# Moving the last two layer norms of the second attention out of its stage, in a four-stage transformer kernel

## The reference

```python
x = layernorm(x + attn1(x))              # no gain or shift, eps 1e-5
# attn1: one head of width 128; Q, K, V from 128x128 weights; out = softmax(Q K^T / s) V
#        out = transpose(out, (0, 2, 1)).reshape(B, S, D); return out @ wo.T
# ffn1, on h = x of the line above:
normed = h * rsqrt(mean(h * h) + 1e-8) * norm_weight
shared = relu(normed @ sw1 + sb1) @ sw2 + sb2                 # 128 -> 512 -> 128
probs  = sigmoid(normed @ router_w.T)                         # 8 experts
w, idx = top_k(probs, 2); w = w / (sum(w) + 1e-6)
routed = sum over experts e of comb[:, e] * (relu(normed @ ew1[e] + eb1[e]) @ ew2[e] + eb2[e])
x = layernorm(h + shared + routed)
```

## Time and profile before

| | |
|---|---|
| three runs, median (lowest to highest) | 1117.27 us (1116.45 to 1118.58) |
| the profiled execution's own time | 1117.38 us |
| its span, first to last instruction | 1115.6 us |
| mean granted TensorE clock | 0.971 of 2.4 GHz |
| busy: PE, DVE, ACT, POOL | 1038.6, 839.0, 652.1, 683.8 us |
| `attend_once` in the trace | about 769 to 877.5 us |
| `mix_experts` in the trace | 878.0 us to the end |

### The profile page before, as it was taken

One profiled execution on the slowest core, in us unless ns is written; L12 is line 12 of the kernel. 1 busy time (PEld: TensorE's weight loads), 2 busy tenths in 40 slices (PEclk: granted clock), 3 DMA queues, 4 the chain that ended last, 5 costly groups with the idle time before them and its releaser, 6 DMA issues. The chain is left out here.

```text
span 1115.6 us, 25325 instructions
## 1 busy us (share of the span) xinstructions
PE 1038.6 (93%) x7983; PEld 855.6 (77%) x7983; DVE 839.0 (75%) x1699; ACT 652.1 (58%) x1319; POOL 683.8 (61%) x663
## 2 busy tenths in 40 slices
PE   6799999999999999999999999687997599999996
PEld 4678888888888888888888888455685477777774
DVE  5877887877787787787787787355765569888896
ACT  4556565565555555656565565454444587766774
POOL 4166876876876876777777786401221277767772
PEclk9999999999999999999999999988898799999998
DMA  5243533533633533534534433110000011212111
GB/s 125 51 97 75 123 85 71 130 78 71 130 79 74 129 78 80 120 78 88 112 78 97 107 75 67 32 42 1 0 1 1 20 60 63 88 56 75 57 38 38
DMA packets 57041, 80.09 MB, mean 72 GB/s; under 512 B 25956, under 2 KB 38048, under 8 KB 55968
## 3 DMA queue, kind: packets, MB, share of 16 engines
q1 hardware_dynamic: 54780, 78.97, 30.0%
q10 hardware_dynamic: 2220, 0.59, 0.3%
HBM read 19.43 MB, written 1.11 MB: 18 GB/s over the span
## 5 line engine op out<-in xcount | busy, mean ns | idle before, releaser
L617 POOL TENSOR_TENSOR probs_lo<-probs 128x512 f16<-128x512 f32 x384 | 420.1, 1108 | 195.2 <-ACT probs L450 193.5
L481 DVE TENSOR_REDUCE maxes<-bank_m 128x1 f32<-128x512 f32 x512 | 353.0, 690 | 138.2 <-PE bank_m L288 134.4
L450 ACT ACTIVATE probs<-bank_s 128x512 f32<-128x512 f32 x512 | 296.9, 608 | 266.1 <-PE bank_s L376 265.3
L369 PE MATMUL bank_s<-qa,ka 128*128 128x512 f32 x512 | 226.0, 441 | 5.7 <-DVE v_parts L528 2.5
L288 PE MATMUL bank_m<-ka,qa 128*128 128x512 f32 x512 | 204.9, 400 | 3.6 <-DMA ka<-tk_lo 3.3
L376 PE MATMUL bank_s<-qb,kb 65*128 65x512 f32 x512 | 205.8, 402 | 2.2 <-DMA qb<-negmax 2.2
L311 PE MATMUL bank_o<-v_now,probs 128*128 128x129 f16 x2048 | 200.6, 220 | 1.0 <-ACT o_parts L416 1.0
L1368 POOL TENSOR_TENSOR hidden_lo<-rectified,hidden_hi 128x512 fp32r<-128x512 f32 x112 | 155.6, 1406 | 60.7 <-ACT hidden_hi L1513 49.9
L311 PEld LDWEIGHTS bank_o<-v_now,probs 128*128 128x128 bf16 x2048 | 175.4, 97 | 21.9 <-issue 20.6
L307 PE MATMUL bank_o<-v_now,probs_lo 128*128 128x65 f16 x2048 | 184.7, 193 | 0.0
L288 PEld LDWEIGHTS bank_m<-ka,qa 128*128 128x128 f32 x512 | 158.6, 310 | 28.6 <-DMA ka<-tk_lo 3.7
(11 more groups left out here) (250 smaller groups left out, 1681.6 us busy)
## 6 DMA issues: line engine op xcount, KB each, us to landing
qa<-tq_hi SPq DMA_DIRECT2D x64, 256.0 KB, 3.8
v_now<-v_parts SPq DMA_DIRECT2D x32, 260.0 KB, 2.3
ka<-tk_hi SPq DMA_DIRECT2D x32, 256.0 KB, 2.9
ka<-tk_lo SPq DMA_DIRECT2D x32, 256.0 KB, 4.9
kb<-tk_hi SPq DMA_DIRECT2D x32, 256.0 KB, 5.0
qb<-tq_lo SPq DMA_DIRECT2D x32, 256.0 KB, 5.2
gates_on_all<-gate_rows SPq DMA_DIRECT2D x8, 1024.0 KB, 4.7
e_raw<-in_L_ffn_ew_dram SPq DMA_DIRECT2D x16, 256.0 KB, 3.0
```

The source lines that it names most:

```text
L369: nc.tensor.matmul(bank_s[u % 2][:], ka[h][:, ks], qa[h][:, qs], start=True, stop=False)
L450: nc.scalar.activation(probs[:, c, u, :], bank_s[u % 2][:], ACT.Exp, scale=SCALE).then_inc(exp_done, 1)
L481: nc.vector.tensor_reduce(maxes[:, j // 2, j % 2:j % 2 + 1], bank_m[j % 2][:], AX.X, ALU.max).then_inc(m_reduced, 1)
L617: nc.gpsimd.tensor_tensor(probs_lo[:, c, u, :], p, hi, ALU.subtract).then_inc(lo_pool, 1)
```

## The change

The work on a chunk's layer norm is cut in four functions, and each part gets another place.

- In step 3 only `times_wo(0)`, `times_wo(1)` and `add_and_sum` (the addition and moments) remain. The roots of chunks 0 and 1 stand on ACT behind the last exponential. `normalise_tokens(0)` and `(1)` stand on DVE in the fifth pass, behind quarters 0 and 1. The normalised `X` is now written by GpSimd, with two 128x512 instructions for a chunk (`normalise_input`), whose second operand is broadcast along the row.
- PE turns chunk 0 of `n_tok` in the fifth pass between its third and fourth quarter, ACT takes it out there, and DVE makes its `nt_lo` last.
- `times_wo`, moments, roots and normalisation of chunks 2 and 3 move to `mix_experts`: PE begins with `times_wo(2)`, turning of chunk 1, `times_wo(3)`. It turns chunks 2 and 3 behind chunks 0 and 1 of ffn 0; DVE, not ACT, takes them out.
- `route()` moves behind chunk 1 and `turn_gates()` behind chunk 3 of ffn 0. The memset of `gates[0]` stands behind the two `normalise_tokens`.
- GpSimd normalises `X` of chunks 2 and 3 behind its work for ffn 0.
- Statistics buffers get a place for each chunk. `o_new`, `w_t`, `nt`, `nt_hi`, `nt_lo` and the semaphores outlive the block.

```diff
@@ attend_once, GpSimd
+            for c in range(EARLY):
+                normalise_input(nc, pool, X, ln, c)
@@ attend_once, PE
-            for c in range(CK // 2, CK):
-                times_wo(c)
+                    if step == STEPS and kt == TB - 3:
+                        turn_tokens(0)
@@ attend_once, ACT
-                    if (step, kt - 1) in FINISH_AT:
-                        root(FINISH_AT[step, kt - 1])
-            for c in range(CK // 2, CK):
-                root(c)
+                    if step == STEPS and kt == TB - 3:
+                        act.wait_ge(ln["n_turned"], 1)
+                        nc.scalar.activation(nt[:, 0:CH], bank_a[0][:], ACT.Copy, scale=nw).then_inc(ln["nt_ready"], 1)
...
+                if step == STEPS - 1:
+                    act.wait_ge(eps_set, 2)
+                    for c in range(EARLY):
+                        root_of_variance(nc, act, ln, c, EPS_RMS)
@@ attend_once, DVE
-                    if (step, kt - 1) in FINISH_AT:
-                        finish(FINISH_AT[step, kt - 1])
-            for c in range(CK // 2, CK):
-                finish(c)
-            dve.wait_ge(x_done, CK)
+                    if (step, kt - 1) in WO_AT:
+                        c = WO_AT[step, kt - 1]
+                        add_and_sum(nc, dve, X, ln, c, bank_m[c % 2])
+                    if step == STEPS and kt in (1, 3):
+                        normalise_tokens(nc, dve, X, persist["n_tok"], ln, kt // 2)
...
@@ mix_experts
-        GATES_AT = 2
+        ROUTE_AT, GATES_AT = 1, 3
+        LATE = CK // 2
@@ mix_experts, GpSimd, after its 16 units of ffn 0
+                if first_ffn:
+                    for c in range(LATE, CK):
+                        normalise_input(nc, pool, X, ln, c)
@@ mix_experts, PE
-                    if first_ffn and c == 0:
+                    if first_ffn and c + 2 < CK:
+                        turn_tokens(c + 2)
+                    if first_ffn and c == ROUTE_AT:
                         route()
...
+            times_wo(LATE)
+            turn_tokens(1)
+            for c in range(LATE + 1, CK):
+                times_wo(c)
             over_ffns(pe, ffn)
@@ mix_experts, ACT
+            act.wait_ge(turned, 2)
+            nc.scalar.activation(nt[:, CH:2 * CH], bank_y[1][:], ACT.Copy, scale=nw).then_inc(nt_ready, 1)
+            take_hi(1)
+            root_of_variance(nc, act, ln, LATE, 1e-8)
...
+                            if c == 0 and f == 1:
+                                root_of_variance(nc, act, ln, LATE + 1, 1e-8)
+                            if c < 2 and f == 3:
+                                take_hi(c + 2)
@@ mix_experts, DVE
+            add_and_sum(nc, dve, X, ln, LATE, bank_y[LATE])
+            take_lo(1)
+            add_and_sum(nc, dve, X, ln, LATE + 1, bank_y[LATE + 1])
+            for c in range(LATE, CK):
+                normalise_tokens(nc, dve, X, n_tok, ln, c)
+            nc.vector.memset(gates[0][:], 1.0).then_inc(gates_in[0], 16)
+            for c in range(LATE, CK):
+                dve.wait_ge(turned, c + 1)
+                nc.vector.tensor_scalar(nt[:, c * CH:(c + 1) * CH], bank_y[c][:], nw, None, ALU.mult).then_inc(nt_ready, 1)
+                take_lo(c)
@@ new
+def normalise_input(nc, pool, X, ln, c):
+    x = X[:, 4 * c:4 * c + 4, :]
+    wide = lambda ap: ap.unsqueeze(2).broadcast_to((P, 4, P))
+    pool.wait_ge(ln["n_ready"], c + 1)
...
+    nc.gpsimd.tensor_tensor(x, x, wide(ln["mv"][:, c, :, 0]), ALU.subtract).then_inc(ln["done"], 1)
+    pool.wait_ge(ln["done"], 2 * c + 1)
+    nc.gpsimd.tensor_tensor(x, x, wide(ln["rstd"][:, c, 0, :]), ALU.mult).then_inc(ln["done"], 1)
```

More of the change, by code:

```diff
@@ L944, in attend_once @@
         o_hi = sb("o_hi", [P, 2, P])
-        o_new = sb("o_new", [P, S])
+        o_new = persist["o_new"]
         bank_a = [ps(f"bank_a{i}") for i in range(4)]
@@ L951, in attend_once @@
         SMALL = small.shape[1]
[L952 to L956, removed]
+        nw = small[:, SMALL - 1:SMALL]
+        ln = persist["ln"]
+        eps, eps_set = ln["eps"], ln["eps_set"]
+        nt, nt_hi, nt_lo = persist["nt"], persist["nt_hi"], persist["nt_lo"]
         shared_hi, shared_lo = sem("shared_hi_ready"), sem("shared_lo_ready")
@@ L1182, in reduce @@
                                             negate=True).then_inc(c_ready, 1)
[L1183 to L1205, removed]
             for n in range(AHEAD):
@@ L1373, in _, with times_wo, turn_tokens @@
         def _(pe):
-            for c in range(CK):
+            def times_wo(c):
+                for j in range(4):
+                    t = 4 * c + j
+                    last = nc.tensor.matmul(bank_y[c][:, j * P:(j + 1) * P], persist["o_new"][:, t * P:(t + 1) * P],
+                                            persist["w_t"][:, 3, :], start=True, stop=True)
+                last.then_inc(ln["y1_filled"], 1)
+            def turn_tokens(c):
+                pe.wait_ge(ln["n_ready"], c + 1)
                 for j in range(4):
@@ L1410, in second_product @@
                     pe.wait_ge(lo_dve, lo_dve_count(n, c))
-                if f == 0 and not first_ffn:
+                if f == 0 and first_ffn:
+                    pe.wait_ge(nt_ready, c + 1)
+                elif f == 0:
                     pe.wait_ge(y_taken, CK * (n - 1) + c + 1)
@@ L1431, in put_input @@
                 pe.wait_ge(comb_t_ready, CK)
+                pe.wait_ge(ln["done"], 2 * CK)
                 pe.wait_ge(y_taken, CK * NE + 2)
@@ L1556, in _, with take_lo @@
             nc.vector.memset(eps[:], 1e-5).then_inc(eps_set, 1)
-            nc.vector.memset(gates[0][:], 1.0).then_inc(gates_in[0], 16)
-            for c in range(CK):
+            def take_lo(c):
                 cs = slice(c * CH, (c + 1) * CH)
@@ L1714, in build @@
         quantised_ffn(nc, a, persist)
+        CK = T // 4
+        persist["o_new"], persist["w_t"] = sb("o_new", [P, B * S], F32), sb("w_turned", [P, 4, P], F32)
+        persist["nt"] = sb("nt", [P, B * S], F32)
+        for which in ("nt_hi", "nt_lo"):
+            persist[which] = sb(which, [P, B * S], F32R)
+        ln = {"stats": sb("ln_attn_stats", [P, CK, 4, 6], F32), "mv": sb("ln_attn_mean_var", [P, CK, 4, 2], F32),
+              "std": sb("ln_attn_std", [P, CK, 2, 4], F32), "rstd": sb("ln_attn_rstd", [P, CK, 2, 4], F32),
+              "eps": sb("attn_eps", [P, 2], F32)}
@@ new lines, in root_of_variance, with normalise_tokens @@
+def root_of_variance(nc, act, ln, c, eps_rms):
+    act.wait_ge(ln["moments"], c + 1)
+    nc.scalar.activation(ln["std"][:, c, 1, :], ln["mv"][:, c, :, 1], ACT.Sqrt, bias=ln["eps"][:, 1:2], scale=1.0 + eps_rms)
+    nc.scalar.activation(ln["std"][:, c, 0, :], ln["mv"][:, c, :, 1], ACT.Sqrt, bias=ln["eps"][:, 0:1]).then_inc(ln["rooted"], 1)
+def normalise_tokens(nc, dve, X, n_tok, ln, c):
+    dve.wait_ge(ln["rooted"], c + 1)
+    nc.vector.reciprocal(ln["rstd"][:, c, :, :], ln["std"][:, c, :, :]).then_inc(ln["inverted"], 1)
+    dve.wait_ge(ln["inverted"], c + 1)
+    for j in range(4):
+        t = 4 * c + j
+        last = nc.vector.tensor_scalar(n_tok[:, t, :], X[:, t, :], ln["mv"][:, c, j, 0:1], ln["rstd"][:, c, 1, j:j + 1],
+                                       ALU.subtract, ALU.mult)
+    last.then_inc(ln["n_ready"], 1)
```

63 lines of the change are left out of this document (41 added, 22 removed).

## The result

The changed kernel took 1109.86 us (median of 5 runs, 1109.72 to 1112.65); the kernel before took 1117.27 us beside it. The ratio is 0.9938, with a 95% interval of 0.9923 to 0.9953: faster by 0.6%, 7.4 us. The forecast was 1109.2 us. One execution of the kernel with both edits, further down, took 5615.5 us and is left out of its time.

The account below looks back on a forecast made before the run. One serial chain from 849.8 to 884.1 us, with PE gaps of 7.26 and 9.47 us, was taken as the bound. 15.9 - 6.8 - 1.0 = 8.1 us off 1117.38 gave 1109.2 us; own range 1107 to 1111.5, with rivals 1104 to 1113.5.

Parts of the forecast that it names:

- Step A: attend_once: fifth pass starts 6.9 us earlier, PE idle some 0.9 us; block ends 15.9 us earlier.
- Rivals 3 and 4: 3: attend_once gains much less, 1116 us, chance 0.08. 4: slow GpSimd broadcast instruction, kernel slower, chance 0.05.
- Step B: Opening of mix_experts: first relu at 4.65 us, ACT starts chunk 1 at 16.4 us from the block's start.
- disputed term: Opening of mix_experts: DVE's normalise_tokens wait out running GpSimd instructions, 3.9 us; chunk 1 at 16.4 instead of 12.6 us.
- Rival 1: DVE meets GpSimd rarely in chunk 0: chunk 1 starts near 12.6 us, loss 3.0 us, total 1105 us; chance 0.22.
- Step C: ffn 0 from chunk 1 through the router: ffn 1 starts 40.7 us after the block's start, loss 6.8 us.
- rival 2: PE's clock falls in ffn 0 behind a 2 to 3 us gap: 3 to 4 us more, 1112.5 us; chance 0.20.
- signs of being wrong: Forecast wrong if the block starts after 864, or ffn 1 more than 43 or less than 38 us behind it.
- the router and GpSimd's pairs: Expected signs: route in ffn 0 at 3.7 us; GpSimd's pairs normalising X at 1.2 to 1.4 us an instruction.
- Step D: ffn 1: GpSimd's four new instructions delay its first hidden_lo; loss 1.0 us, between 0 and 2.

Follow-up runs that it names:

- kernel with both edits: Changed kernel with gates memset at the expert block's front and GpSimd's remainders behind the last normalise_tokens: 1102.5 us, again 1105.41 us.
- roots back: Changed kernel with the roots of chunks 0 and 1 back in step 3 and normalise_tokens right behind each moment set: 1116.01 us, ratio 0.9992.
- GpSimd-waits run: Changed kernel with one added wait: GpSimd begins the shared expert's remainders only when all n_tokens are normalised: 1102.52 us, again 1100.92 us.
- warm-products run: Changed kernel with 15 extra unused 512-column products in PE's gap inside chunk 1 of the shared expert: 1109.66 us, ratio 0.9912.
- memset-first run: Changed kernel with DVE's memset of the first gates moved to the front of the expert block: 1105.26 us, ratio 0.9883.
- first-stage-only run: Changed kernel with chunks 2 and 3 finished at the end of attend_once, router and gates behind chunks 0 and 2 again: 1109.56 us, ratio 0.9919.

## Why the prediction was right, and where it was lucky

The sum was 15.9 - 6.8 - 1.0 = 8.1 us; the spans differ by 7.7 us, which the table splits as 1.1 + 17.5 - 10.65 - 0.25.

**Step A** came out at 17.5 instead of 15.9 us. The mechanism is shown: roots back, and 7.9 us of it are gone with PE's gap. PE restarts with 0.43 us idle and keeps its clock. The 1.6 us too little are a size: I added durations end to end, while in the rows most DVE instructions start about 0.1 us before the one ahead of them ends (854.31 + 1.84 = 856.15, the next starts at 856.07), over a dozen in a row, and I started 0.3 us late. GpSimd's broadcast instruction took 1.04 to 1.07 us here, less than the 1.27 us taken. Rivals 3 and 4 are out.

**Step B** has its disputed term shown. I forecast 3.9 us of waiting for GpSimd and chunk 1 at 16.4 us; it was 6.2 us for what takes 2.2 us alone, and 16.6 us. The GpSimd-waits run took the waiting away and nothing else of DVE. Rival 1 is out. What I put at nothing is the clock at the block's start: behind PE's wait of 3.62 us the opening ran at 1.2 GHz, and the first relu came at 6.0 us instead of 4.65. In the roots-back kernel, whose clock was up there, it came at 4.6 us; there DVE waits 1.1 instead of 2.0 us for its first `bank_y`, and chunk 1 starts at 15.3 us. So the low clock cost 1.3 us, and it hid in a step that came out nearly right because my allowance for DVE's waits took it in.

**Step C** is where the sum failed: 27.9 us from chunk 1 to ffn 1 instead of 24.3. From chunk 1's first relu to the router it was 7.7 us instead of 5.3, and from the router's start to the next product 4.9 instead of 3.7 us. That is rival 2, which I gave 0.20 and priced at 3 to 4 us; the warm-products run, with the clock held, has 5.1 us in place of the 7.7. I had the gap at 2 to 3 us and called it too short, since the only gap with a fall behind it that I showed was 7.26 us. It was 3.76 us, and in the memset-first run the clock fell behind 1.77 us. By one of my own signs of being wrong, ffn 1 more than 43 us behind the block's start, the forecast was wrong here: it was 44.5 us. The block's start (859.5 instead of 861 to 863 us), the router and GpSimd's pairs lay outside what I had named too.

**Step D** was 1.4 us (1.0 forecast): from ffn 1's first product to ffn 2's it is 24.2 us instead of 22.8, of which 0.84 us is the one long wait, and the kernels in which GpSimd doesn't have this work there need 22.8 to 22.9 us. The rest of the span grew by only 0.25 us, because the time from PE's last instruction to the end is 9.3 us instead of 10.2 in every changed kernel, and the six networks between are 0.3 us shorter together. I had neither, and no run explains them.

So the forecast of 1109.2 us is right by mechanism in A and D and in the disputed term of B, and by luck in its nearness: 3.9 us too little loss in ffn 0 and 0.4 us in step D were met by 1.6 us in step A, 1.1 us in code that wasn't changed, and 1.2 us behind ffn 1. One judgement in it was not tested before the result: that the late part pays. I had it, over A and the rest, as 8.1 us net without splitting it by part. The first-stage-only run shows that the two halves are far from equal.

## What to carry to other kernels

Price a change part by part against leaving the part out, not only in sum: here putting the roots and normalisation of two chunks back takes the whole gain away, and an elaborate late stage, as built, gives back all that it wins. Before moving DVE work into a stage, look at what GpSimd does there. If GpSimd has slack, letting it wait for DVE's short serial piece can be worth more than the overlap (one wait removed 4.0 us of waiting, and ffn 1 came 7.3 us sooner). A gap of PE can cost its length and then the low clock behind it: keep constant work such as a memset out of the path that feeds PE (3.0 us up to ffn 1 by itself, nothing that the times can tell on top of the wait). Read a trace as one execution, and look at the times and clocks of the others before a microsecond is put down to an edit.

## What was not expected of the hardware

- A GpSimd 128x512 instruction with a broadcast second operand took 1.04 to 1.10 us in six of the eight cases in the changed kernel and 1.5 us in the other two; the one with two full fp32 operands took 1.27 us. Rows of the changed kernel:

```profile
904.54 1.49 POOL L1800 TENSOR_TENSOR x_tokens<-x_tokens,ln_attn_mean_var 128x512 f32<-128x512 f32 x1
...
907.75 1.04 POOL L1800 TENSOR_TENSOR x_tokens<-x_tokens,ln_attn_mean_var 128x512 f32<-128x512 f32 x1
```

- After a gap of 1.77 us PE ran partly at the low clock (0.60 of 2.4 GHz from 873 to 877); after 1.15 us in the GpSimd-waits run and 1.22 us in the changed kernel it did not.
- The 32 small router products, at 8 columns each and with PE busy throughout, are followed or cut by the low clock in every trace looked at. Two traces of the same kernel agree on how far the router gets (3.74 us both times in one, 5.8 us both times in another that reaches the router 0.3 us sooner), while the times and clocks of that other kernel's unprofiled executions differ.
